# Count stage: the item offsets of a set are read between the items and the last two old-count additions of the set before it

## The reference, cut to what matters

```python
edge_index = jnp.stack([src, dst])
h = jnp.maximum(_layernorm(x), 0.0); x = x + _L0_gnn_ref(h, ..., src, dst)          # attention over edges
h = jnp.maximum(_layernorm(x), 0.0); x = x + _L1_gnn_ref(h, ..., edge_weight, edge_index)
h = jnp.maximum(_layernorm(x), 0.0); x = x + _L2_gnn_ref(h, src, dst, ...)
h = jnp.maximum(_layernorm(x), 0.0); x = x + _L3_gnn_ref(h, edge_index, ...)
```

## Time and profile before

| what | value |
|---|---|
| time of the kernel, median of 3 runs | 1293.65 us (1293.31 to 1293.77) |
| time of the profiled execution | 1290.73 us |
| its span, first to last instruction | 1288.6 us |
| part of the span that the 80 sets take on TensorE | 29.06 to 358.8 us |
| TensorE busy, share of the span | 1040.7 us, 81% |
| VectorE busy | 967.3 us, 75% |
| ScalarE busy | 692.3 us, 54% |
| GpSimd busy | 598.5 us, 46% |

### The profile page before, as it was taken

One profiled execution on the slowest core, in us unless ns is written; L12 is line 12 of the kernel. 1 busy time (PEld: TensorE's weight loads), 2 busy tenths in 40 slices (PEclk: granted clock), 3 DMA queues, 4 the chain that ended last, 5 costly groups with the idle time before them and its releaser, 6 DMA issues.

```text
span 1288.6 us, 23338 instructions
## 1 busy us (share of the span) xinstructions
PE 1040.7 (81%) x8352; PEld 615.1 (48%) x8352; DVE 967.3 (75%) x1603; ACT 692.3 (54%) x903; POOL 598.5 (46%) x343
## 2 busy tenths in 40 slices
PE   3877777777795888888888888882799699999893
PEld 2545545544452222222222222221469699999783
DVE  8668888897764999999999999981865654542566
ACT  7555566556534997999989999980000000001221
POOL 8542453232001998999999899996000000000000
PEclk9988888999987998999999999996799899999996
DMA  0010000000027111121111222211000100010201
GB/s 10 28 39 5 5 9 5 6 7 16 1 63 213 35 36 46 44 54 41 42 47 45 51 54 50 53 41 46 1 1 32 37 29 21 2 33 8 71 25 38
DMA packets 98907, 44.80 MB, mean 35 GB/s; under 512 B 85196, under 2 KB 96716, under 8 KB 98672
## 3 DMA queue, kind: packets, MB, share of 16 engines
q1 hardware_dynamic: 97104, 41.58, 12.2%
q0 software_dynamic: 1696, 1.74, 0.5%
HBM read 30.73 MB, written 12.56 MB: 34 GB/s over the span
## 4 chain that ended last, share of the span: by engine, by line
PE 51%; DVE 25%; issue 11%; ACT 5%; POOL 5%; another core or an unknown queue 2%; DMA 2%; SPq 1%; DVEq 0%; ACTq 0%; POOLq 0%
PE PS L1325 16%; DVE Eb L1150 16%; PE PS L553 10%; PE PS L557 8%; POOL Eb L982 3%; PE PS L1765 3%; DVE Eb L1144 3%; PE PS L1333 2%; PE PS L1074 2%; ACT Eb L1115 2%; PE PS L1064 2%; PE PS L1316 1%; ACT Eb L1117 1%; PE PS L1772 1%
## 5 line engine op out<-in xcount | busy, mean ns | idle before, releaser
L982 POOL TENSOR_SCALAR Eb<-Eb 128x1024 f32<-128x1024 f32 (+4 forms) x175 | 431.2, 2486 | 77.1 <-ACT Eb L1119 75.8
L1150 DVE SCALAR_TENSOR_TENSOR Eb<-Eb,PS 128x1024 f32<-128x1024 f32 (+4 forms) x350 | 366.6, 1084 | 18.0 <-ACT Eb L1117 11.7
L1119 ACT ACTIVATE Eb<-PS,small 128x1024 f32<-128x1024 f32 (+2 forms) x263 | 251.7, 998 | 28.9 <-PE PS L1064 25.2
L593 ACT ACTIVATE CT<-PS 128x500 f32 x313 | 183.6, 587 | 141.2 <-PE PS L557 132.6
L553 PE MATMUL PS<-mov,oneS 128*128 128x100 f16 x1565 | 182.2, 226 | 79.6 <-issue 74.0
L553 PEld LDWEIGHTS PS<-mov,oneS 128*128 128x128 f16 x1565 | 144.7, 104 | 157.9 <-issue 111.5
L1325 PE MATMUL PS<-hs,CT 128*128 128x192 f16 (+1 forms) x2500 | 213.9, 247 | 3.5 <-DVE SG L1566 1.6
L1325 PEld LDWEIGHTS PS<-hs,CT 128*128 128x128 f16 (+1 forms) x2500 | 208.4, 99 | 7.4 <-DVE SG L1566 2.3
L1064 PE MATMUL PS<-Qb,Kb 96*128 96x512 f16 (+3 forms) x700 | 184.5, 367 | 10.4 <-ACT Eb L1119 6.7
L1074 PE MATMUL PS<-Eb,V 128*25 128x512 f32 (+3 forms) x1400 | 172.6, 566 | 3.4 <-DVE Eb L1150 1.8
L435 DVE TENSOR_TENSOR oneS<-iotaX,KL 128x2560 f16<-128x2560 int16 x80 | 120.8, 1510 | 68.7 <-PE PS L557 67.0
(11 more groups left out here) (278 smaller groups left out, 1007.2 us busy)
## 6 DMA issues: line engine op xcount, KB each, us to landing
Kb<-kd SPq DMA_DIRECT2D x168, 96.0 KB, 2.3
qd<-QH SPq DMA_DIRECT2D x12, 192.0 KB, 2.9
kd<-QH SPq DMA_DIRECT2D x12, 192.0 KB, 3.2
hs<-t_d SPq DMA_DIRECT2D x12, 192.0 KB, 2.5
Qb<-qd SPq DMA_DIRECT2D x4, 384.0 KB, 3.9
CT<-x_d SPq DMA_DIRECT2D x1, 1200.0 KB, 9.1
x_d<-B SPq DMA_DIRECT2D x6, 192.0 KB, 1.9
t_d<-A SPq DMA_DIRECT2D x6, 192.0 KB, 1.9
```

The source lines that it names most:

```text
L593: a.activation(K.CT[:, :, bass.ds(words[g % 4][0], GI * W)], K.bank(g % 4)[:, 0:25 * GI * W].rearrange("p (a c) -> p a c", a=25), ACT.Copy ...
L982: g.tensor_scalar(e, e, ELO, None, ALU.max).then_inc(S("floored"), 1)
L1119: a.activation(e, ps, ACT.Exp, scale=K.unsc[0:r, :]).then_inc(S("score_read"), 1)
L1150: v.scalar_tensor_tensor(out=e, in0=e, scalar=EHI, in1=cn, op0=ALU.min, op1=ALU.mult).then_inc(S("weighed"), 1)
```

## The change

The groups of a set are no longer handled one after the other to the end. The first two groups are as before: five items and the old-count addition, each. Then come the items of the third and fourth group, ten matmuls in a row. Then TensorE's sequencer reads the 20 offsets of the next set. Only then come the old-count additions of the third and fourth group, one right behind the other. The additional transposes of a set come after these, as before. The wait for the next set's one-hot matrices stands in front of its first item. The registers with the first offsets of the third and fourth group stay in use over the read. The work itself is the same: the same items, additions and reads, in the same banks. ScalarE's and VectorE's programs are not changed.

```diff
-    for g in PRESENT:
-        s, o = g // 4, GI * (g % 4)
-        if g % 4 == 0:
-            words = vals = to = None
-            words = load_windows(K, t, mybir.EngineType.PE, s, 1)
-            t.wait_ge(S("one_hot"), s + 1)
-        vals = words[g % 4]
-        ps = bank(g % 4)[:, 0:25 * GI * W].rearrange("p (a c) -> p a c", a=25)
+    def items(g, vals):
+        s, o, ps = g // 4, GI * (g % 4), group_bank(g)
         for k in range(GI):
             to = ps[:, :, 0:W] if k == 0 else ps[:, :, bass.ds(vals[k], W)]
             t.matmul(to, K.oneS[:, s % DEEP, o + k, :], ...
                      start=(k == 0), stop=False, skip_group_check=True)
+
+    def add_old(g, first):
         if g >= 2:
             t.wait_ge(S("placed"), INDEX[g - 2] + 1)
-        t.matmul(ps, K.identb[:, :], K.CT[:, :, bass.ds(vals[0], GI * W)], start=False, stop=True, ...
-                 ).then_inc(S("counted"), 1)
-        if g == PRESENT[-1] or g // 4 != PRESENT[INDEX[g] + 1] // 4:
+        t.matmul(group_bank(g), K.identb[:, :], K.CT[:, :, bass.ds(first, GI * W)], start=False, stop=True,
+                 skip_group_check=True).then_inc(S("counted"), 1)
+
+    words = load_windows(K, t, mybir.EngineType.PE, 0, 1)
+    for s in range(SETS):
+        groups = [g for g in range(4 * s, 4 * s + 4) if g in INDEX]
+        t.wait_ge(S("one_hot"), s + 1)
+        for g in groups[:2]:
+            items(g, words[g % 4])
+            add_old(g, words[g % 4][0])
+        for g in groups[2:]:
+            items(g, words[g % 4])
+        left = [(g, words[g % 4][0]) for g in groups[2:]]
+        words = None
+        if s + 1 < SETS:
+            words = load_windows(K, t, mybir.EngineType.PE, s + 1, 1)
+        for g, first in left:
+            add_old(g, first)
+        left = first = None
         ...
```

More of the change, by code:

```diff
@@ L542, in build_tensor, with group_bank @@
     t.wait_ge(S("zero_a"), 2)
-    for g in PRESENT:
-        s, o = g // 4, GI * (g % 4)
-        if g % 4 == 0:
-            words = vals = to = None
-            words = load_windows(K, t, mybir.EngineType.PE, s, 1)
-            t.wait_ge(S("one_hot"), s + 1)
-        vals = words[g % 4]
-        ps = bank(g % 4)[:, 0:25 * GI * W].rearrange("p (a c) -> p a c", a=25)
+    def group_bank(g):
+        return bank(g % 4)[:, 0:25 * GI * W].rearrange("p (a c) -> p a c", a=25)
+    def items(g, vals):
+        s, o, ps = g // 4, GI * (g % 4), group_bank(g)
         for k in range(GI):
@@ L554, in build_tensor @@
                      start=(k == 0), stop=False, skip_group_check=True)
+    def add_old(g, first):
         if g >= 2:
             t.wait_ge(S("placed"), INDEX[g - 2] + 1)
-        t.matmul(ps, K.identb[:, :], K.CT[:, :, bass.ds(vals[0], GI * W)], start=False, stop=True, skip_group_check=True
-                 ).then_inc(S("counted"), 1)
-        if g == PRESENT[-1] or g // 4 != PRESENT[INDEX[g] + 1] // 4:
[L560 to L567, removed]
+        t.matmul(group_bank(g), K.identb[:, :], K.CT[:, :, bass.ds(first, GI * W)], start=False, stop=True,
[16 more added lines that the diff above has]
+        left = first = None
+        if s == SUM_AT:
+            sums(2)
+        if s == SLOTS_AT:
+            windows(2)
+        if s in TURN_AT:
+            turn_items(TURN_AT[s])
+        if SOFT_AT.get(s) in SOFT_TURN:
+            soft_turn(*SOFT_TURN[SOFT_AT[s]])
     t.wait_ge(S("counted"), len(PRESENT))
```

## The result

The changed kernel takes 1323.52 us (median of 4 runs, 1321.8 to 1324.53), against 1293.68 us for the kernel before in the same comparison. The ratio is 1.0239, with a 95% interval of 1.0223 to 1.0256. It is 29.8 us slower; 32 us were forecast.

What follows compares the result with a forecast made beforehand. TensorE's sequencer was taken as the limit. 77 x (0.78 x 0.45 + 0.22 x 0.36) = 33.1 us, less 1.4, plus 0.3, makes 32 us: 1293.65 + 32 = 1325.7 us, range over all 1310 to 1342.

Steps and rivals of the forecast that it cites:

- The bound: Count stage: TensorE's sequencer sets the pace, 1.36 us of read and four groups of about 0.66 us, 4.0 us a set.
- The read moves and hides nothing: Read of 20 offsets, now behind ten items: keeps its 1.36 us on the sequencer; costed at nothing at 2.4 GHz.
- The round trip: Addition 3, placement, next set's addition 1: takes 1.22 us against 0.78 us of issuing, so 0.45 us late at 2.4 GHz.
- One of the signs named in the prediction: In each set's profile after: 0.2 to 0.5 us of TensorE idle in front of addition 1, ended by the placement.
- The sets at 1.2 GHz: Count-stage sets at the lower clock: 0.66 us for late addition 1 less 0.30 us of vanished waits, 0.36 us more each.
- The wait holds the sequencer: At addition 1 the sequencer itself waits, so all items behind and the next read move back by the whole 0.45 us.
- the reciprocal: VectorE's 5.03 us softmax piece sets the pace for about three sets, hiding their new stall: a discount of 1.4 us.
- 0.3 more for the clock: Count stage: more idle time may bring the lower clock somewhat more often; ten points would cost 1.6 us, 0.3 added.
- the forecast's own range: Whole kernel's time if the forecast case holds: 1314 (a stall of 0.3 us) to 1335 us, chance 0.73.
- Addition 2: Its wait for group 4's placement, ending 0.62 us or so after the first, just fits 0.66 us of issuing; no cost.
- The one-hot matrices: Rival: VectorE's lead shrinks to 0.9 us, some ten sets stall TensorE by up to 1 us; 1297 to 1304, chance 0.05.
- The rival of the lower clock: Nearly all count-stage sets run at 1.2 GHz, 4.65 us each against 4.06: 45 us more, 1339 us; chance 0.12.

Runs made afterwards that it cites:

- the far dependence: Old-count additions read zeros and wait for no placement two back, in both orders: 1297.03 us in the changed order, 1294.17 us in the order of the kernel before.

## Why the prediction was right

**The bound.** At 2.4 GHz the sequencer sets the pace of the stage. The reads of 30 offsets showed this from the other side: they lengthened the stage by their own additional 139 us and 24 more. At 1.2 GHz the prediction read the rows wrongly. Between two reads it is the array that sets the pace there: TensorE is busy for 3.72 of 3.72 us, and additions stay 0.83 us apart even where no placement is waited for. The 0.62 us of five items in the earlier trace rows overlap with the additions on both sides, so they do not show room in the array; the starts of the additions do.

**The read moves and hides nothing.** Shown by the profile after, at 2.4 GHz: 1.32 us of idle time in front of addition 3, and a read that starts at 203.1, when the last of the ten items is already in the array (they end at 203.28). At 1.2 GHz a part of the read is hidden, but that was so before the change too: the idle time was 0.61 us before, and is 0.97 us after.

```profile
205.48 0.76 PE L553 MATMUL PS<-mov,oneS 128*128 128x100 f16 x5 [0.61 <-issue]
```

**The round trip.** Shown. It was taken from sets 77 and 78 of the kernel before as 1.22 and 1.44 us. After the change it takes 1.23 us at 2.4 GHz, and the whole set 4.43 us, where 3.99 + 0.45 = 4.44 was forecast. With the dependence moved further back, or with the read between additions 3 and 1, the loss is gone, and with the clock held at 0.98 it is 33.7 us, 0.44 us for a set, where 0.45 us were taken. One of the signs named in the prediction did not hold as it was put: idle time in front of addition 1 stands in the waits only 45 times (18.1 us), not in each set, since at 1.2 GHz the array is still at work when the sequencer waits.

**The sets at 1.2 GHz: the right number from two wrong terms.** Such a set takes 4.66 us, and 4.65 were forecast: 4.29 before, 0.66 more for the late addition 1, 0.30 less for waits that go away. Neither term is what happened. The 0.66 us set the round trip of 1.44 us against the 0.78 us that issuing needs, but the array alone needs 1.23 us from addition 3 to addition 1 at this clock, and with the dependence it took 1.43 (172.63 to 174.06): late by 0.20. And the additions 0.81 us apart were not held up by placements, as the far dependence showed, so there were no 0.30 us to win back; the sequencer did wait for placements there, but behind a busy array. What has grown is the idle time under the read, by the 0.36 us between 0.61 and 0.97. With the far dependence it differs between the orders too (0.77 us in front of the items at 207.47 in the order before, 1.19 us in front of 111.55 in the order after), so at least a part of the 0.36 us belongs to the order and not to the dependence; how it divides was not measured. That the two errors cancelled is luck.

**The wait holds the sequencer.** The last address computation of the items in front starts at 205.1, that of the late addition at 205.7, after the placement's end at 205.11 + 0.59 = 205.70. It is the same all through the stage: in 74 of the 76 sets from 1 to 76, the address computation of addition 1 starts within 0.06 us of the end of the placement that it waits for. Had the sequencer gone past it, the array would have caught up, and the set could not have grown by the full wait. The rule of the Trainium skill, "Perfetto Trace Analysis", section "Tensor Engine Instruction (MATMUL, LD_WEIGHTS)", that a matmul waits for its semaphore in a queue while its sequencer goes on, does not reach this wait. In the trace the semaphore `placed` stands at the address computation, which the sequencer executes itself, and the matmul behind it carries no wait. By that rule the set would, by my estimate, have stayed near 3.99 us, where 4.43 were measured.

**Where the sum was off.** 77 x 0.430 = 33.1 us, less 1.4 for the reciprocal and 0.3 more for the clock, was set against 35.4 us measured in the stage. The mis-sized term is the lower clock. I had left its share at 22% and added 0.3 us. The granted clock of 0.75 makes the share 50%. With it the sum is 0.50 x 4.43 + 0.50 x 4.66 = 4.545 us for a set, 0.49 more than the 4.06 of before, and 77 x 0.49 = 37.7, less 1.4, is 36.3 us. The 1.4 us were not measured by themselves. The profiled executions still lie 32.15 us apart, where 32 were forecast, and this is the luck of the later stages, 3 us shorter in this execution. The medians lie 29.8 us apart, because the profiled execution of before was 2.9 us below its median and that of the changed kernel 0.6 us below. The lower end of the forecast's own range is 1315 by its working (1293.65 + 23.1 - 1.4), not 1314.

**Addition 2.** It was costed at nothing, and that was right: no idle time stands in front of 206.49. The reason was partly wrong. I took ScalarE's second placement to end 0.62 us or more behind the first; it is 0.47 us (1.06 us for two, 0.59 for one). This left more room than I thought, and it is a reason why the run with all additions late cost 18 us and not 24 or more.

**The rivals.** The one-hot matrices did not come late: TensorE waited for them for 2.6 us in all, 5.0 before, and the stall of note is that behind the reciprocal, 1.72 us against 3.16 before.

```profile
289.01 0.70 PE L551 MATMUL PS<-mov,oneS 128*128 128x100 f16 x5 [1.72 <-DVE mov L435]
```

The earlier number held the 1.05 us of a read, so VectorE's part went from 2.1 us to 1.7. The rival of the lower clock came true in part, half of the sets' time and not nearly all of it.

## What to carry to other kernels

Before instructions are put behind others to cover a stall, ask what the moved ones released. Here they released a placement that the next set needs, and the stall that they were moved behind had been the cover of that round trip. For the same reason, splitting the moved pair around the read took the whole loss back. Ask also at which clock each stretch of the trace ran: at 2.4 GHz the sequencer was the limit here, at 1.2 GHz, between two reads, the array, and a distance between two instructions that looks like a wait at one clock may be work at the other. A trip between engines that a change will bring close together can often be read in the old trace, at the end of a loop, where a short iteration already runs it bare. And where a sequencer sets the pace, a read of many registers costs nearly its full length wherever it stands; measure its price for the size and place wanted before counting on it.

## What the runs showed of the hardware that I had not expected

A read of 20 words into TensorE's registers took 1.36 us at the median of 80 and 1.55 us at most. A read of 30 words took 2.36 us as a rule when it began at word 0 or 60 of its row of the table, and 7.08 us, three times as long, when it began at word 30 or 90. The reads of 20, which begin at every twentieth word, show no such alternation. The words have 4 bytes, so the slow reads begin at 120 and 360 bytes and the fast ones at 0 and 240; whether alignment is the cause was not tested.

Two placements of ScalarE whose banks are both ready end 0.47 us apart, though each is shown as 0.59 us long.

With additional matmuls the granted clock of the stage rose from 0.87 to 0.98 in the order with the read between the additions, and nothing measurable changed. In the changed order it rose from 0.75 to 0.98 and came with a stage 5 us shorter. There the additions' way through the array is part of the round trip: from the start of addition 3 to the start of its placement it is 0.51 us at 2.4 GHz (204.60 to 205.11) and 0.72 us at 1.2 GHz (172.63 to 173.35).
